# A five-layer graph network kernel: inputs loaded in small parts, own edges added by TensorE, the norm's low pieces by VectorE

## The chip, the cores and the metric

One core of a Trainium2 chip runs the whole program in one launch. The metric is the time of one execution on the device in microseconds (us), as the median of several runs. The core has five engines that run in parallel and meet at semaphores: TensorE (PE; its weight loads are shown apart as PEld), VectorE (DVE), ScalarE (ACT), GpSimd (POOL) and SyncE (SP, which here issues most of the DMAs).

## The reference, cut to what matters

```python
def _gin_conv(x, src, dst, edge_attr, w1, b1, bn_w, bn_b, w2, b2, ew, eb):
    edge_emb = edge_attr @ ew.T + eb
    n = x.shape[0]                                            # 3125 nodes, 128 features
    agg_x = jax.ops.segment_sum(x[src], dst, num_segments=n) + x
    agg_e = jax.ops.segment_sum(edge_emb, dst, num_segments=n) + eb
    h = jnp.concatenate([agg_x, agg_e], axis=1)
    h = h @ w1.T + b1                                         # 256 hidden
    mean = jnp.mean(h, axis=0)
    var = jnp.mean((h - mean) ** 2, axis=0)
    h = (h - mean) * jax.lax.rsqrt(var + BN_EPS) * bn_w + bn_b
    h = jax.nn.relu(h)
    return h @ w2.T + b2

h = jnp.maximum(_layernorm(x, axis=-1), 0.0)
for l in range(5):                                            # 103125 edges, sorted by dst, 16 attributes each
    h = _gin_conv(h, src, dst, edge_attr, W1[l], B1[l], BNW[l], BNB[l], W2[l], B2[l], EW[l], EB[l])
    if l < 4:
        h = jax.nn.relu(h)
return x + h
```

The `+ x` in `agg_x` is an edge of every node to itself on top of the listed ones. The text calls these the own edges.

## The kernel before

The kernel turns the edge list into a dense matrix of counts, `adj` (source node in 25 tiles of 128 rows, destination node in 3150 columns, bf16), and then aggregates by matrix products. The build comes first, in one block of the program, and is what the change touches. The five layers come after it and are not touched.

**Strips.** The columns of `adj` are built in 175 strips of 18 columns (`SC`), six groups of three columns each. For strip `u`, DVE makes two one-hot tables from the edge keys (`one_hots`, which calls `equal`, L421: a 128x768 form for the low part of the source node, a 128x456 form for the rest). PE multiplies them in six products into one of three PSUM banks (`counts`, L800). ACT copies the bank to `adj` (L935). The one-hot tables have two slots, so DVE's tables of strip `u` wait until PE's counts of strip `u-2` are done.

**Steps.** The edge attributes are summed by destination in 74 steps (`attr_step`, L824: 11 products, 22 instructions, since they are float32). DVE makes a one-hot table for each (`dst_one_hots`, L613). Step `u+6` (`LEAD`) is done in strip `u`, so the steps fill strips 0 to 67. The attributes lie in SBUF by 25 parts `k` of three steps each. Three times in each of seven chunks of 450 columns PE also splits the sums into pieces (L435, L439).

**The first norm.** ACT sums the rows of `x` (L962) from strip 7 on, squares from strip 20, and normalises from strip 36. Each group of four node tiles then gets a high piece in float16 (ACT, `high_piece`, L915) and a low piece, which is the value less the high piece (POOL, `low_piece`, L549, six of them; a seventh small one is DVE's, L745).

**Own edges and overflow.** POOL adds the identity to `adj` where a strip crosses the diagonal (`add_own`, L556, 31 pieces, bf16 from and to SBUF). It also adds the counts of overfull groups (`add_overflow`, L570, 14 of them). The first layer's aggregation (`agg0_products`, L430) is spread over strips 68 to 173 as 150 steps of a node tile each, one or two in a strip, and its last chunk runs after the last strip. It waits for both additions.

**Loading.** SP issues the DMAs in the order of its code. The attributes come in five parts (`ATTR_PARTS`), of 2, 2, 5, 7 and 9 of the 25 `k`, the node features `x` in one of 24 tiles and one for the rest, and all of it, with the weights, is issued without a wait once the first keys are loaded. After that SP stores the group starts (L478, L480), reads them back (L484), stores and reads the picks of the overfull groups (L486, L488), and loads the edge order for a check (L491). POOL issues the indirect gathers of edge rows and pairs (L528, L535).

The instructions of DVE, PE, ACT and POOL stand in the order of the code, strip by strip, so an engine that waits holds up all that is behind it.

## Time and profile before

| | |
|---|---|
| median of 3 runs | 686.85 us (686.78 to 686.87) |
| the profiled execution's own time | 684.61 us |
| its span, first to last instruction | 682.8 us |
| mean granted TensorE clock | 0.959 of full speed |

The profile is of one execution. Its span is 1.8 us shorter than its time, and its time is 2.2 us below the median of the three runs. Times in the rows are in microseconds from the span's start, and a busy PE is not PE at its peak. The build takes the first 245 us, the layers the rest.

### The profile page before, as it was taken

The numbers are of one execution on the slowest core, as the hardware profiler recorded it, in microseconds if no ns is written. First come the engines' busy times: TensorE is split into PE (matmuls) and PEld (weight loads), VectorE is DVE, ScalarE is ACT, GpSimd is POOL, SyncE is SP. The second block draws the span as 40 slices with busy tenths as digits, with TensorE's granted clock in tenths as the row PEclk, the third lists the DMA queues.
The fourth block names the chain that finished last, engine by engine and source line by source line (L and its number), as shares of the span: only waits on it lengthen the run. The fifth ranks groups of instructions, "written<-read, shape, count | busy, mean of one in ns | idle before, by whom it ended". The sixth has DMA issues, their size and how long they took to land.

```text
span 682.8 us, 13708 instructions
## 1 busy us (share of the span) xinstructions
PE 618.4 (91%) x5319; PEld 383.1 (56%) x5319; DVE 345.8 (51%) x837; ACT 262.5 (38%) x569; POOL 61.8 (9%) x90
## 2 busy tenths in 40 slices
PE   4788898988999979799997999997999998999976
PEld 3676677754555534755554755556655548555546
DVE  6788999989999937612112521204412125210124
ACT  1266966755666624701013510106201027010133
POOL 5640032410110100000000000000000000000000
PEclk9788999999999999999998999999999998999998
DMA  6961000000000000010000100000100000100033
GB/s 183 324 205 8 3 28 3 5 5 4 4 3 5 4 4 3 1 32 1 1 0 1 31 0 0 0 0 0 30 0 0 0 0 0 32 1 2 0 94 95
DMA packets 13305, 18.97 MB, mean 28 GB/s; under 512 B 2263, under 2 KB 7397, under 8 KB 13251
## 3 DMA queue, kind: packets, MB, share of 16 engines
q1 hardware_dynamic: 12099, 16.00, 7.7%
q0 software_dynamic: 1152, 2.20, 1.4%
q8 instruction: 40, 0.66, 0.4%
q14 instruction: 14, 0.11, 0.1%
HBM read 16.26 MB, written 1.60 MB: 26 GB/s over the span
## 4 chain that ended last, share of the span: by engine, by line
PE 57%; DVE 3%; ACT 1%; issue 1%; POOLq 0%; DVEq 0%
PE bank L1275 38%; PE bank L1338 10%; PE bank L1310 7%; PE bank L1304 2%; DVE bn_stats L1497 1%; ACT h L1391 1%; DVE h L1518 0%; ACT aggT L1382 0%; DVE h L1519 0%; PE bank L230 0%; ACT bn_small L1404 0%; PE bank L1321 0%; DVE h L1538 0%; DVE bound_row L1477 0%; DVE bn_small L1512 0%
## 5 line engine op out<-in xcount | busy, mean ns | idle before, releaser
L1275 PE MATMUL bank<-adj,h_pieces 128*128 (+1 forms) x1372 | 265.4, 353 | 0.0
L1275 PEld LDWEIGHTS bank<-adj,h_pieces 128*128 128x128 f16 x1372 | 133.1, 97 | 131.6 <-issue 8.7
L1497 DVE BATCH_NORM_STATS2 bn_stats<-bank 128x6 f32<-128x450 f32 (+1 forms) x70 | 43.8, 629 | 228.7 <-PE bank L1310 224.8
L935 ACT ACTIVATE adj<-bank 128x450 bf16<-128x450 f32 x175 | 96.0, 549 | 78.0 <-PE bank L800 63.2
L1382 ACT ACTIVATE aggT<-bank 128x450 f32<-128x450 f32 x28 | 15.3, 546 | 270.6 <-PE bank L1310 237.9
L421 DVE TENSOR_TENSOR h<-iota_lo,h 128x768 bf16<-128x768 bf16 (+1 forms) x182 | 101.6, 558 | 5.8 <-PE bank L800 4.4
L824 PE MATMUL bank<-h,adj 128*17 128x40 f32 (+11 forms) x1752 | 84.2, 207 | 15.7 <-DVE h L613 9.6
L824 PEld LDWEIGHTS bank<-h,adj 128*17 128x17 f32 x1752 | 73.0, 104 | 23.2 <-DVE h L613 13.2
L800 PEld LDWEIGHTS bank<-h 128*128 128x128 bf16 x1064 | 51.7, 100 | 60.6 <-DVE h L421 46.3
L800 PE MATMUL bank<-h 128*128 128x75 bf16 x1064 | 70.3, 203 | 16.6 <-DVE h L421 14.6
L430 PE MATMUL bank<-adj,h_pieces 128*128 128x450 bf16 x343 | 83.6, 356 | 1.6 <-issue 1.6
L1338 PE MATMUL bank<-weights,h 128*128 128x128 f32 (+1 forms) x500 | 65.8, 299 | 18.7 <-DVE h L1519 18.7
L1338 PEld LDWEIGHTS bank<-weights,h 128*128 128x128 f32 (+1 forms) x500 | 64.1, 212 | 22.8 <-issue 17.8
L421 DVE TENSOR_TENSOR h<-iota_a,key_a 128x456 bf16<-128x456 bf16 (+1 forms) x182 | 75.3, 414 | 0.0
L613 DVE TENSOR_TENSOR h<-h,adj 128x440 f32<-128x440 f32 x74 | 45.7, 619 | 8.3 <-remote 6.4
L1310 PE MATMUL bank<-aggT,weights 128*128 128x450 f32 x112 | 47.3, 544 | 1.0 <-ACT aggT L1382 1.0
L1391 ACT ACTIVATE h<-bank,weights 128x450 f32 (+1 forms) x70 | 41.4, 635 | 13.8 <-DVE bn_stats L1497 13.0
L1399 ACT ACTIVATE h<-h,bn_small 128x512 f32<-128x512 f32 (+1 forms) x65 | 44.3, 744 | 4.5 <-DVE bn_small L1513 4.5
L1525 DVE TENSOR_TENSOR h<-bank,weights 128x512 f32<-128x512 f32 x30 | 20.7, 691 | 34.6 <-PE bank L1338 34.6
L430 PEld LDWEIGHTS bank<-adj,h_pieces 128*128 128x128 f16 x343 | 27.3, 98 | 15.5 <-issue 3.1
L1310 PEld LDWEIGHTS bank<-aggT,weights 128*128 128x128 f32 x112 | 20.8, 189 | 15.7 <-issue 10.6
L556 POOL TENSOR_TENSOR adj<-adj,ident 128x128 bf16<-128x128 bf16 (+13 forms) x31 | 14.3, 466 | 116.8 <-ACT adj L935 116.8
(147 smaller groups left out, 323.1 us busy)
## 6 DMA issues: line engine op xcount, KB each, us to landing
adj<-attr SPq DMA_DIRECT2D x1, 2524.5 KB
adj<-attr SPq DMA_DIRECT2D x1, 1963.5 KB
weights<-wpack SPq DMA_DIRECT2D x5, 323.0 KB
out<-h SPq DMA_DIRECT2D x6, 256.0 KB
adj<-attr SPq DMA_DIRECT2D x1, 1402.5 KB, 6.8
adj<-attr SPq DMA_DIRECT2D x2, 561.0 KB
h<-mpack SPq DMA_DIRECT2D x5, 179.0 KB
adj<-order SPq DMA_DIRECT2D x2, 202.0 KB
```

The source lines that it names most:

```text
L421: return nc.vector.tensor_tensor(out.rearrange("p (j c t) -> p j c t", j=j, t=2), pairs.unsqueeze(1).to_broadcast([P, j, n // 2, 2]), key. ...
L430: last = nc.tensor.matmul(bank[:, 0:CW], hp[:, k, s, :], adj[:, k, ds(c * CW, CW)], start=(k == 0 and s == 0), stop=stop and s == pieces_o ...
L613: V.tensor_tensor(dst_oh[:, i % DST_SLOTS, :].rearrange("p (q w) -> p q w", q=RUN), iota_d.unsqueeze(1).to_broadcast([P, RUN, DW]), rel_d[ ...
L800: last = nc.tensor.matmul(cnt_ps[n % CNT_BANKS][:, g * AW:(g + 1) * AW], lo[:, g * P:(g + 1) * P], a[:, g * AP:g * AP + AW], start=(g == 0 ...
L824: last = nc.tensor.matmul(att_ps[c % 2][0:REC, a - c * CW:b - c * CW], attr_i[:, k, t * REC:(t + 1) * REC], dst_oh[:, i % DST_SLOTS, q * D ...
L935: nc.scalar.activation(out_view(u), bank_view(n % CNT_BANKS), ACT.Copy).then_inc(s_ev, 1)
L1275: last = nc.tensor.matmul(agg_ps[b][:, 0:CW], hp[:, k, s, :], adj[:, k, ds(c * CW, CW)], start=(k == 0 and s == 0), stop=stop and s == pie ...
L1310: nc.tensor.matmul(w1_ps[b][h][:, 0:CW], wp[:, W1A + h * P:W1A + (h + 1) * P], sums_in, start=False, stop=True).then_inc(w1_done, 1)
L1338: last = nc.tensor.matmul(w2_ps[u % 2][0:r, j * P:(j + 1) * P], h1[:, h, a:a + r], wp[:, W2T + h * P:W2T + (h + 1) * P], start=(h == 0), s ...
L1391: last = nc.scalar.activation(h1[:, h, ds(c * CW, CW)], w1_ps[b][h][:, 0:CW], ACT.Identity, bias=wp[:, B1 + h:B1 + h + 1])
L1399: last = nc.scalar.activation(v, v, ACT.Relu, bias=shift[:, h:h + 1], scale=scale[:, h:h + 1])
L1497: V.bn_stats(stats[:, h, ds(c * 6, 6)], w1_ps[b][h][:, 0:cols]).then_inc(st_last if last and h == 1 else st_done, 1)
```

## The change

The attributes are loaded in 13 parts of two `k` each (the last of one), each issued 12 steps ahead of its first use and behind a wait for that step. `x` is loaded in four parts of six tiles, at steps 6, 8, 10 and 12. The stores of the group starts come after step 24's part, the picks after strip 32's work, and the weights after all attribute parts. The own edges are one or two more products of PE in every strip: the identity times a shifted cut of a padded identity, 18 columns, accumulated into the same bank before ACT copies it. The six low pieces are DVE's, each two strips after its high piece. POOL has neither of the two any more.

```diff
-ATTR_PARTS = ((0, 2), (2, 4), (4, 9), (9, 16), (16, 25))
+ATTR_PARTS = [(k, min(k + 2, NODE_TILES)) for k in range(0, NODE_TILES, 2)]
+X_PARTS = ((0, 6), (6, 12), (12, 18), (18, 24))
-ORDER_AFTER = 9
+ORDER_AFTER, ATTR_AHEAD, X_EVERY, STARTS_AFTER = 9, 12, 2, 24
...
-        ident = sb(whole, "ident", [P, P], BF16)
+        ident_pad = sb(whole, "ident", [P, 2 * SC + P], BF16)
+        ident = ident_pad[:, SC:SC + P]
...
                     sp.wait_ge(s_pair[0], 16)
-                    attr_rows(2)
                     sp.wait_ge(s_zero, 1)
-                    sp.dma_start(x_st[:, 0:NODE_TILES - 1, :],
-                                 x[0:(NODE_TILES - 1) * P, :].rearrange("(k p) f -> p k f", p=P)).then_inc(s_x, 16)
                     sp.dma_start(x_st[0:LAST_ROWS, NODE_TILES - 1, :],
-                                 x[(NODE_TILES - 1) * P:N_NODES, :]).then_inc(s_x, 16)
-                    for m in range(3, len(ATTR_PARTS)):
-                        attr_rows(m)
+                                 x[(NODE_TILES - 1) * P:N_NODES, :]).then_inc(s_x[-1], 16)
+                    parts = 2
+                    for i in range(STEPS):
+
+                        if parts < len(ATTR_PARTS) and i == max(3 * ATTR_PARTS[parts][0] - ATTR_AHEAD, 0):
+                            if i > 0:
+                                sp.wait_ge(s_step, i)
+                            attr_rows(parts)
+                            parts += 1
+                        for j in range(len(X_PARTS)):
+                            if i == LEAD + X_EVERY * j:
+                                sp.wait_ge(s_step, i)
+                                x_rows(j)
+                        if i == STARTS_AFTER:
+                            store_starts()
+                        if i == PICK_AT + LEAD:
+                            spread_picks()
                     sp.dma_start(wp[:, :], wpack[0]).then_inc(l_wp, 16)
                     sp.dma_start(mp, mpack[0]).then_inc(l_mp, 16)
...
-                        if c == CHUNKS - 1:
-                            add_own(len(PIECES_OWN) - 1)
                         pool.wait_ge(s_ev, max(strip_at((c + 1) * CSTRIPS - 1), overflow_at(c)) + 1)
-                        pool.wait_ge(s_own, own_before(c))
...
-                        if u >= NORM_AT + 4 and (u - NORM_AT) % 4 == 0 and (u - NORM_AT) // 4 < UNITS:
-                            low_piece((u - NORM_AT) // 4 - 1)
-                        while n < len(PIECES_OWN) - 1 and PIECES_OWN[n][2] <= (u + 1) * SC:
-                            add_own(n)
-                            n += 1
...
+                        i = (u - NORM_AT - 6) // 4
+                        if (u - NORM_AT - 6) % 4 == 0 and 0 <= i < UNITS - 1:
+                            dve.wait_ge(s_hi, i + 1)
+                            V.tensor_tensor(units(hp, i)[:, :, 1, :], units(x_st, i), units(hp, i)[:, :, 0, :],
+                                            ALU.subtract).then_inc(hp_done, 1)
...
+                        if own is not None:
+
+                            to = cnt_ps[n % CNT_BANKS][:, 0:SG * AW].rearrange("p (g k m) -> p g k m", g=SG, m=GW)
+                            for k in range(own * SC // P, min((own * SC + SC - 1) // P, NODE_TILES - 1) + 1):
+                                at = SC + own * SC - k * P
+                                last = nc.tensor.matmul(to[:, :, k, :], ident, ident_pad[:, at:at + SC], start=False, stop=True,
+                                                        skip_group_check=True)
                         last.then_inc(s_cnt, 1)
...
-                        counts(strip_at(u), SG)
+                        counts(strip_at(u), SG, u)
...
                             if k == 0:
-                                pe.wait_ge(s_own, own_before(c))
                                 pe.wait_ge(s_ov, OV * (c + 1))
...
-                            if k == 0:
-                                act.wait_ge(s_x, 32)
+                            for j, (a, _) in enumerate(X_PARTS):
+                                if k == a:
+                                    act.wait_ge(s_x[j], 32 if j == len(X_PARTS) - 1 else 16)
```

SP's queue before, from its second attribute part to the picks:

```order
L457 DMA adj<-attr 128x2x561
L457 DMA adj<-attr 128x5x561
L467 DMA adj<-x 128x24x128
L469 DMA adj<-x 53x128
L457 DMA adj<-attr 128x7x561
L457 DMA adj<-attr 128x9x561
L473 DMA weights<-wpack 128x646
L474 DMA h<-mpack 128x358
L478 DMA starts<-start_index 60x1
L480 DMA starts<-start_index 126x1 x8
L484 DMA h<-starts 7x150 x2
```

The same queue now; the rows from the second of `adj<-attr 128x2x561 x2` on stand behind waits for steps:

```order
L442 DMA adj<-attr 128x2x561
L471 DMA adj<-x 53x128
L442 DMA adj<-attr 128x2x561 x2
L452 DMA adj<-x 128x6x128 x3
L442 DMA adj<-attr 128x2x561
L452 DMA adj<-x 128x6x128
L442 DMA adj<-attr 128x2x561 x2
L456 DMA starts<-start_index 60x1
L458 DMA starts<-start_index 126x1 x8
L462 DMA h<-starts 7x150 x2
L442 DMA adj<-attr 128x2x561 x2
```

The large transfers are cut up and spread, the stores of the starts stand behind more of them, and the weights behind all.

PE's queue before, in the part where the first layer's products (L430) share it with the counts (L800):

```order
L430 MATMUL bank<-adj,h_pieces 128x450 x4
L800 MATMUL bank<-h 128x75 [waits counts_evacuated,onehots_made]
L800 MATMUL bank<-h 128x75 x5
L430 MATMUL bank<-adj,h_pieces 128x450 x2
L800 MATMUL bank<-h 128x75 [waits counts_evacuated,onehots_made]
```

And now, where L783 is the counts, L791 the own edges and L415 the first layer:

```order
L783 MATMUL bank<-h 128x75 [waits counts_evacuated,onehots_made]
L783 MATMUL bank<-h 128x75 x5
L791 MATMUL bank<-ident 128x6x3
L415 MATMUL bank<-adj,h_pieces 128x450 x4
L783 MATMUL bank<-h 128x75 [waits counts_evacuated,onehots_made]
L783 MATMUL bank<-h 128x75 x5
L791 MATMUL bank<-ident 128x6x3 x2
L415 MATMUL bank<-adj,h_pieces 128x450 x2
```

Each strip has one own product more, and two where it crosses from one node tile to the next.

On DVE, around strip 42, where the first of the six low pieces (L724) now stands between a step's one-hots (L591) and the next strip's (L409):

```order
L409 TENSOR_TENSOR h<-iota_lo,h 128x768
L409 TENSOR_TENSOR h<-iota_a,key_a 128x456
L591 TENSOR_TENSOR h<-h,adj 128x440
L724 TENSOR_TENSOR h_pieces<-adj,h_pieces 128x4x128
L409 TENSOR_TENSOR h<-iota_lo,h 128x768
L409 TENSOR_TENSOR h<-iota_a,key_a 128x456
```

Before, the row L724 was not there and the others stood the same.

## Rows read from the trace of the kernel before

**Rows 1.** The page, busy time of each engine over the span.

```profile
PE 618.4 (91%) x5319; PEld 383.1 (56%) x5319; DVE 345.8 (51%) x837; ACT 262.5 (38%) x569; POOL 61.8 (9%) x90
```

**Rows 2.** Stretches: length, then busy time (instructions) of each engine, clock, DMA share, GB/s.

```profile
18.00:62.00 44.00, 36.51 (x590) 28.53 (x591) 34.53 (x97) 20.56 (x75) 19.85 (x17) 0.78 0.71 200
62.00:144.00 82.00, 73.27 (x1469) 60.87 (x1470) 79.59 (x195) 61.69 (x172) 19.93 (x21) 0.95 0.03 9
144.00:245.00 101.00, 91.81 (x976) 48.82 (x976) 96.83 (x244) 64.32 (x123) 12.83 (x30) 0.98 0.01 4
28.00:32.00 4.00, 2.25 (x24) 1.47 (x24) 0.00 (x0) 0.00 (x0) 2.62 (x3) 0.62 1.05 314
```

**Rows 3.** Waits of DVE from 17 to 245 us: total, times, longest.

```profile
DVE h L613 <- remote: 6.4, 2, 4.3
DVE h L421 <- PE bank L800: 4.4, 10, 0.9
DVE h L613 <- PE bank L824: 1.9, 3, 0.6
DVE h L421 <- issue: 1.0, 1, 1.0
```

**Rows 4.** Timeline, DVE's two long waits: start, duration, and idle before.

```profile
32.06 0.62 DVE L613 TENSOR_TENSOR h<-h,adj 128x440 f32<-128x440 f32 x1 [4.29 <-remote]
...
56.49 0.62 DVE L613 TENSOR_TENSOR h<-h,adj 128x440 f32<-128x440 f32 x1 [2.06 <-remote]
```

**Rows 5.** Groups of DVE by form, 17 to 245 us: busy, mean ns, idle before.

```profile
L421 DVE TENSOR_TENSOR h<-iota_lo,h 128x768 bf16<-128x768 bf16 x175 | 99.6, 569 | 5.4 <-PE bank L800 4.0 <-issue 1.0
L421 DVE TENSOR_TENSOR h<-iota_a,key_a 128x456 bf16<-128x456 bf16 x175 | 73.7, 421 | 0.0
```

**Rows 6.** Line L639 on the overflow keys: ns minimum/median/maximum of two.

```profile
L639 DVE TENSOR_SCALAR h<-h,picked_start_and_first x2: 270/747/1224, 105.5 to 105.7; 7x128 f32<-7x128 int32 x2
```

**Rows 7.** Timeline, DVE beside POOL's low piece, and beside an overflow addition.

```profile
100.39 1.43 POOL L549 TENSOR_TENSOR h_pieces<-adj,h_pieces 128x512 f16<-128x512 f32 x1 [7.95 <-ACT h_pieces L915]
...
100.75 1.32 DVE L421 TENSOR_TENSOR h<-iota_a,key_a 128x456 bf16<-128x456 bf16 x1
...
154.46 0.52 DVE L421 TENSOR_TENSOR h<-iota_a,key_a 128x456 bf16<-128x456 bf16 x1
```

**Rows 8.** Timeline of DVE, then of PE, two strips of the late part.

```profile
188.42 0.55 DVE L421 TENSOR_TENSOR h<-iota_lo,h 128x768 bf16<-128x768 bf16 x1
188.89 0.39 DVE L421 TENSOR_TENSOR h<-iota_a,key_a 128x456 bf16<-128x456 bf16 x1
189.20 0.55 DVE L421 TENSOR_TENSOR h<-iota_lo,h 128x768 bf16<-128x768 bf16 x1
...
188.79 0.92 PE L430 MATMUL bank<-adj,h_pieces 128*128 128x450 bf16 x4
189.55 0.37 PE L800 MATMUL bank<-h 128*128 128x75 bf16 x6
189.76 0.54 PE L430 MATMUL bank<-adj,h_pieces 128*128 128x450 bf16 x2
```

**Rows 9.** Timeline of DVE, one step's one-hots and what follows.

```profile
98.44 0.62 DVE L613 TENSOR_TENSOR h<-h,adj 128x440 f32<-128x440 f32 x1
98.98 0.55 DVE L421 TENSOR_TENSOR h<-iota_lo,h 128x768 bf16<-128x768 bf16 x1
```

**Rows 10.** Group of PE's counts, 17 to 245 us.

```profile
L800 PE MATMUL bank<-h 128*128 128x75 bf16 x1064 | 70.3, 203 | 16.6 <-DVE h L421 14.6 <-issue 0.8
```

**Rows 11.** Group of PE's counts' weight loads, 17 to 245 us.

```profile
L800 PEld LDWEIGHTS bank<-h 128*128 128x128 bf16 x1064 | 51.7, 100 | 60.6 <-DVE h L421 46.3 <-issue 3.7
```

**Rows 12.** Timeline of SP's queue: the starts stored, and read back; DVE's first use.

```profile
49.11 0.35 SPq L478 DMA_DIRECT2D starts<-start_index  x1
...
63.82 0.62 SPq L484 DMA_DIRECT2D h<-starts  x2
...
83.17 0.30 DVE L655 TENSOR_TENSOR h<-h 7x150 f32<-7x150 int32 x1
```

**Rows 13.** Timeline, end of the build: POOL's last own piece, overflow, PE's last chunk.

```profile
243.59 0.33 POOL L556 TENSOR_TENSOR adj<-adj,ident 128x78 bf16<-128x78 bf16 x1 [2.90 <-ACT adj L935]
244.17 0.75 POOL L570 TENSOR_TENSOR adj<-adj,h 128x75 bf16 x2 [0.24 <-POOL adj L556]
245.02 9.48 PE L430 MATMUL bank<-adj,h_pieces 128*128 128x450 bf16 x49 [1.60 <-issue]
```

More of the change, by code:

```diff
@@ L157, in ln_tiles @@
     return range(2 * (u - at), min(2 * (u - at) + 2, NODE_TILES)) if at <= u else ()
-def diag_pieces():
-    pieces = []
-    for k in range(NODE_TILES):
-        a, end = k * P, min((k + 1) * P, COLS)
-        while a < end:
-            b = min(end, (a // CW + 1) * CW)
-            pieces.append((k, a, b))
-            a = b
-    return pieces
 def agg0_steps(u):
@@ L378, in gin_program @@
             s_attr = [sem(f"attr_rows{m}_loaded") for m in range(len(ATTR_PARTS))]
-            s_x = sem("x_loaded")
+            s_x = [sem(f"x{j}_loaded") for j in range(len(X_PARTS))]
             s_zero = sem("x_pad_zeroed")
@@ L463, in _, with x_rows, store_starts @@
                     attr_rows(1)
+                    def x_rows(j):
+                        a, b = X_PARTS[j]
+                        sp.dma_start(x_st[:, a:b, :], x[a * P:b * P, :].rearrange("(k p) f -> p k f", p=P)).then_inc(s_x[j], 16)
+                    def store_starts():
+                        sp.wait_ge(s_start, BLOCKS)
+                        sp.dma_start(starts[0:BLOCK0].rearrange("(p b) -> p b", b=1), start_i[0:BLOCK0, 0:1]).then_inc(s_sdram, 16)
+                        for b in range(1, BLOCKS):
+                            sp.dma_start(starts[base_of(b):base_of(b) + GB].rearrange("(p b) -> p b", b=1),
+                                         start_i[0:GB, b:b + 1]).then_inc(s_sdram, 16)
+                        sp.wait_ge(s_sdram, 16 * BLOCKS)
+                        for at, out in ((0, first_e), (1, next_e)):
+                            sp.dma_start(out, starts[at:at + GROUPS].rearrange("(c j) -> c j", c=CHUNKS)).then_inc(s_ranges, 16)
@@ L473, in _ @@
+                    assert parts == len(ATTR_PARTS)
                     sp.dma_start(wp[:, :], wpack[0]).then_inc(l_wp, 16)
                     sp.dma_start(mp, mpack[0]).then_inc(l_mp, 16)
[L477 to L481 removed]
@@ L791, in transposes, with counts @@
                         last.then_inc(s_tr, 1)
-                    def counts(n, tiles):
+                    def counts(n, tiles, own=None):
                         pe.wait_ge(s_oh, n + 1)
```

40 lines of the change are left out of this document (8 added, 32 removed).

## The prediction

> **What bounds the kernel now.** I read the page's busy times first [rows 1], and they mislead: PE is busy 91% of the span, but most of that is in the layers, which the change leaves alone. So the view that counts is the table of stretches over the build, the first 245 us [rows 2]. From 62 to 144 us DVE is busy 79.59 of 82 us, from 144 to 245 us 96.83 of 101 us, while PE has 73.27 and 91.81. DVE sets the pace of the strips, and PE follows close behind. From 18 to 62 us it is otherwise: DVE has only 34.53 of 44 us, and the DMA share is 0.71. The list of DVE's waits says what it lacks there [rows 3]: 6.4 us in two waits that the profile calls remote, at 27.8 and 54.4 us in the timeline [rows 4]. Both are waits for PE's step, and PE itself waits there for nothing that the profile shows. From 28 to 32 us the DMA engines have no time free (share 1.05, 314 GB/s), PE gets 24 products done in 4 us, and DVE and ACT none [rows 2].
>
> So there are three kinds of time to be had or lost: the two stalls, what makes DVE's own instructions long, and PE's distance from being the bound.
>
> **Smaller parts in the queue.** Term A is the first stall. It costs 4.29 us [rows 4]. The clock then falls to the lower of its levels (0.62 in that stretch [rows 2], so partly at 1.2 GHz), and the knock-on is one wait of 1.0 us called issue and one of the three waits on L824, 0.6 us [rows 3]: 5.9 us. The change takes away what coincides with it. The parts now issued before strip 0 are 561 KB each in place of the 1.4 MB (5 `k`), 1.6 (`x`), 2.0 (7) and 2.5 (9) in one go, and nearly all behind a step. I take the stall as gone, −5.9 us; the other bound is 0, since the coincidence is all that the rows show.
>
> A page of the Trainium skill speaks against this cause: Runtime: NRT & Kernel Launch, section Instruction fetch mechanics, says that an engine streams its own instructions ahead by a DMA queue and that the cost of crossing a block is mostly hidden. By that the full DMA engines would not starve PE of instructions; the dribble of 24 products in 4 us [rows 2] does not fit a hidden fetch, but no row names it either. That is the rival "the stalls stay" below.
>
> Term B is the second stall, 2.06 us [rows 4] with a knock-on of about 0.5 us of the waits on L800 and 0.6 us on L824 [rows 3]: 3.2 us. It falls when SP stores the group starts, from 49.11 us on [rows 12], with the large transfers over. The change moves those stores some four strips later but doesn't remove them. Nothing tells me whether the stall goes; I take half, −1.6 us, with 0 and −3.2 as bounds.
>
> What the queue moves: the starts are stored after step 24 (strip 18), where before they went with strip 14. Store to read-back takes 63.82 − 49.11 = 14.7 us; DVE's first use is at 83.17 us [rows 12]. Strip 18's step ends at about 57 us [rows 4], so 26 us are left for these 14.7 and a landing: no wait. Every attribute part has 12 steps of at least 1.3 us each ahead of it (0.54 us for the step's one-hots [rows 9] and 0.78 for the strip's [rows 8]), against a transfer of 561 KB, 2 us at the rate of [rows 2]. Strips 18 to 32 take (83.17 − 56.49) / 14 = 1.9 us each [rows 4, 12], so the part due at step 30 goes out behind the store at about step 32 and has 10 steps left. The weights are needed only after the last strip. Cost 0, covered by that distance.
>
> **POOL's work leaves.** Term C. A DVE instruction that meets a POOL one that reads and writes SBUF gets longer: beside the low piece the 128x456 one-hot took 1.32 us [rows 7] in place of 0.39 [rows 8]. How much in all follows from the groups [rows 5] less the undisturbed durations [rows 8]: 99.6 − 175 × 0.55 = 3.35 us for the one form, 73.7 − 175 × 0.39 = 5.45 us for the other. L639 adds 1.22 − 0.27 = 0.95 us [rows 6]. That is 9.75 us. The 14 overflow additions stay, each 0.52 − 0.39 = 0.13 us [rows 7, 8], 1.8 us. So −8.0 us, on the engine that sets the pace. The bounds are −8.5 (L613 is stretched too now and then) and −5, if PE, which is co-bound in the late part, takes a part of it.
>
> **The low pieces on DVE.** The trace has no such instruction on DVE. The nearest is L613, float32 in SBUF, two inputs, 440 columns: the next starts 98.98 − 98.44 = 0.54 us after it [rows 9]. For 512 columns that is 0.54 × 512 / 440 = 0.63, less for the fixed part: 0.60 us, six times 3.6 us. Each waits for ACT's high piece, two strips earlier. The first one here begins at 100.39 − the 0.6 us of the high piece on ACT, and ends where POOL starts, 100.39 [rows 7]; DVE comes to that place at 98.98 + 1.3 = 100.3 us [rows 9], so 0.1 us of wait, and it is about the same or nothing at the others: 0.3 us in all. Together +3.9 us; bounds 3.0 and 6.
>
> **Own edges on PE.** Term D. 197 products more, 77 in strips 0 to 67 and 120 after. Their price has no row. The counts, also 128x128 bf16 weights, go at (189.76 − 189.55) / 6 = 0.035 us each with 75 columns [rows 8]; the own ones have 18 columns but load weights too, so I take 0.04. The upper bound is the whole duration of one, 0.203 us [rows 10]. In the late part PE's work in a strip is 0.21 us of counts and, with 294 products over 106 strips at (189.55 − 188.79) / 4 = 0.19 us, 0.53 us: 0.74 us against DVE's 189.20 − 188.42 = 0.78 us [rows 8]. With 1.13 × 0.04 it is 0.78 as well. The two engines are then level, and because one strip has four products and the next two, with only two one-hot slots between the engines, part of it shows. I take half of 120 × 0.04 = 4.8 us, 2.4 us, and a fifth of 77 × 0.04 early, where DVE has more in a strip: 0.6. Together +3.0 us; bounds 0 and 10.
>
> The Trainium skill would price this higher: TensorE: Matmul & The Clock Gate, section LDWEIGHTS, gives a weight load as its columns over 1.2 GHz, an estimate of 107 ns for 128 columns. By the page 0.107 would stand where I have 0.04, and the sum would come out nearly 7 us higher, since the groups' mean of 100 ns for a load [rows 11] overlaps the products but this price would not. Here six loads and products took 0.21 us together [rows 8], so the trace speaks against using it as a cost of each.
>
> **The end.** PE's last chunk waits for the overflow addition, which waits for the last own piece: from 243.59 to 244.17 us [rows 13]. −0.6 us.
>
> **Sum.** −5.9 − 1.6 − 8.0 + 3.9 + 3.0 − 0.6 = −9.2 us. The profiled execution took 684.61 us by its own time, so 675.4; it lies 2.24 us below the median of 686.85, and against that median the forecast is 677.6.
>
> **The rivals.**
> 1. *The forecast*, the sum above with B at either end: 676 to 679.3 by B alone. Chance 0.5.
> 2. *The stalls stay.* For: B falls without large transfers, so full DMA engines can't be the one cause of both, and PE's waits have no releaser. Against: the DMA share of 1.05 in the first. −9.2 + 5.9 + 1.6 = −1.7: 685.2. Chance 0.18.
> 3. *PE becomes the bound.* The own products cost p each, and PE's strip passes DVE's. The exposed cost is about 120p − (0.78 − 0.74) × 106 late and 77p − 5 early (0.08 us of room in 68 strips). Without them the sum is −12.2 us. At p = 0.1 that is 7.8 + 2.7 = 10.5 and the time is 685.2. Slower than before from p = 0.11 on; at the bound of 0.203 it would be 30.7 us, 705. For: PE is level with DVE already [rows 2]. Against: 0.035 us a product [rows 8]. Chance 0.09, of which 0.06 slower.
> 4. *All of it.* Both stalls go and PE's work is hidden: −9.2 − 1.6 − 3.0 = −13.8: 673.1. For: removing 2.9 us and more of stretched one-hots lets both engines flow. Chance 0.17.
> 5. *The queue is late.* SP stands in its store of the starts, or a part behind it lands late, and DVE or PE waits some 3 us: 680.6. The 11 us of distance speak against it. Chance 0.06.
>
> **How the numbers follow.** The likeliest is 677.6 us. From 672.5 to 685.3 the range takes in cases 1, 4 and 5 and the centres of 2 and of 3 at p = 0.1, and leaves out the slower end of 3 and the tails, under 0.2. A measurement of this kernel tells about 0.2% from no change, 1.4 us. Case 2 lies on the edge of that, so I give it 0.07 for no change, with 0.02 from the others: faster 0.84, same 0.09, slower 0.07.
>
> **What the profile would show.** A: from 20 to 45 us DMA share well under 1, no idle of DVE over 2 us before strip 7, and the clock not at its lower level there. B: whether a wait of DVE of about 2 us called remote is left when the starts are stored. C: the one-hots at 0.55 and 0.39 us on the mean, except beside 14 overflow additions; low pieces at 0.6 us. D: own products 0.04 us apart, DVE's waits for PE's counts up from 4.4 us by 2 to 3, strips in the late part still 0.78 to 0.83 us. The end: PE's wait before its last chunk 1.0 in place of 1.6 us. The layers take the same time as before. I would be wrong if PE's dribble has another cause than the transfers, or if the own products' price is 0.1 us.

## The result and the profile after

The changed kernel takes 684.22 us (median of 11 runs) beside 688.26 us for the kernel before on the same chip: a ratio of 0.9949, with a 95% interval of 0.9925 to 0.9973. In three more batches of runs the two kernels were timed side by side, and the ratios were 0.9935 [0.9913, 0.9956], 0.9950 [0.9927, 0.9972] and 0.9952 [0.9927, 0.9976]. (A batch here is a set of runs of several kernels taken together on one chip, with the kernel before among them; the recorded texts say "call". Times are compared within a batch.) So the change makes the kernel faster by half a per cent, some 3.5 us, where 9.2 us were forecast.

The page's busy times of the changed kernel, to be laid beside [rows 1]:

```profile
PE 621.1 (91%) x5516; PEld 394.6 (58%) x5516; DVE 341.2 (50%) x843; ACT 263.4 (39%) x569; POOL 43.3 (6%) x53
```

POOL has lost 18.5 us of work, and DVE, which has taken over six low pieces, is busy 4.6 us less than before all the same. The table of stretches of the same kernel, with the columns of [rows 2]:

```profile
18.00:62.00 44.00, 38.31 (x667) 31.82 (x668) 36.12 (x102) 23.16 (x84) 18.06 (x15) 0.81 0.45 128
62.00:144.00 82.00, 74.70 (x1520) 62.71 (x1521) 77.93 (x203) 61.72 (x169) 11.32 (x6) 0.96 0.19 54
144.00:245.00 101.00, 93.57 (x1070) 54.76 (x1069) 92.81 (x237) 62.25 (x119) 4.69 (x10) 0.97 0.02 4
28.00:32.00 4.00, 1.94 (x28) 1.38 (x27) 1.81 (x4) 1.09 (x3) 2.07 (x3) 0.73 0.59 180
```

The last line is the one to look at. The DMA share from 28 to 32 us has fallen from 1.05 to 0.59, as forecast, and still PE gets only 28 products done in those 4 us, against 24 before. PE's timeline there, with the idle time before each group and what ended it:

```profile
26.96 0.26 PE L814 MATMUL bank<-h,adj 128*17 128x28 f32 x4 [0.48 <-issue]
27.68 0.29 PE L814 MATMUL bank<-h,adj 128*17 128x24 f32 x5 [0.46 <-issue]
28.43 0.28 PE L814 MATMUL bank<-h,adj 128*17 128x20 f32 x5 [0.46 <-issue]
29.18 0.29 PE L814 MATMUL bank<-h,adj 128*17 128x24 f32 x5 [0.47 <-issue]
```

Five products, a gap of 0.46 us in which PE waits for nothing that the profile shows, and again: one round every 0.74 us. The text calls this a dribble. It is the first stall, still there. DVE's waits from 17 to 245 us, as in [rows 3]:

```profile
DVE h L409 <- PE bank L791: 6.0, 14, 1.2
DVE h L591 <- PE bank L814: 3.5, 5, 0.8
DVE h L591 <- remote: 3.2, 2, 1.8
DVE h L409 <- remote: 0.9, 1, 0.9
...
DVE h L409 <- PE bank L783: 0.6, 1, 0.6
```

They add up to 14.2 us, where those of [rows 3] add up to 13.7. The one wait of 4.29 us [rows 4] is cut up into four of 0.6 to 1.8 us between 26 and 34 us, but the total over the build hasn't moved. What did move is the length of DVE's instructions, in its groups by form (compare [rows 5]; L724 are the low pieces):

```profile
L409 DVE TENSOR_TENSOR h<-iota_lo,h 128x768 bf16<-128x768 bf16 x175 | 97.0, 554 | 7.5 <-PE bank L791 5.6 <-remote 0.9 <-PE bank L783 0.6
L409 DVE TENSOR_TENSOR h<-iota_a,key_a 128x456 bf16<-128x456 bf16 x175 | 68.6, 392 | 0.0
...
L724 DVE TENSOR_TENSOR h_pieces<-adj,h_pieces 128x512 f16<-128x512 f32 x6 | 4.1, 684 | 0.0
```

And the end of the build on PE (compare [rows 13]), with the first product of the layers:

```profile
240.38 9.49 PE L415 MATMUL bank<-adj,h_pieces 128*128 128x450 bf16 x49 [0.93 <-POOL adj L556]
255.24 0.91 PE L1294 MATMUL bank<-edge_sums,edge_weights 102*128 102x450 bf16 x2 [5.37 <-issue]
```

The last chunk begins 4.64 us earlier than before (245.02 us). But then PE stands still for 5.37 us before the layers' first product, where the kernel before stood still for 2.32. That row of the kernel before reads:

```profile
256.82 0.54 PE L1304 MATMUL bank<-edge_sums,edge_weights 102*128 102x450 bf16 x2 [2.32 <-POOL ones L1433]
```

So 3.05 us of the build's gain are given back at the border between the two blocks of the program, and only 1.58 us are left where the layers begin.

### The profile page after: what moved, and what is told of

It reads as the page before. It is cut to its first block, busy times and chain, and to the rows that moved or that the text cites. A ratio compares the mean times of both kernels' runs of the same rounds, so it can differ in the third digit from the quotient of the medians.

```text
span 683.5 us, 14077 instructions
## 1 busy us (share of the span) xinstructions
PE 621.1 (91%) x5516; PEld 394.6 (58%) x5516; DVE 341.2 (50%) x843; ACT 263.4 (39%) x569; POOL 43.3 (6%) x53
## 4 chain that ended last, share of the span: by engine, by line
PE 58%; DVE 3%; ACT 1%; issue 1%; POOLq 0%; DVEq 0%
PE bank L1265 38%; PE bank L1328 10%; PE bank L1300 7%; PE bank L1294 2%; DVE bn_stats L1487 1%; ACT h L1381 1%; DVE h L1508 0%; ACT aggT L1372 0%; DVE h L1509 0%; PE bank L220 0%; ACT bn_small L1394 0%; PE bank L1311 0%; DVE h L1528 0%; DVE bound_row L1467 0%; DVE bn_small L1502 0%
## 5 line engine op out<-in xcount | busy, mean ns | idle before, releaser
L409 DVE TENSOR_TENSOR h<-iota_lo,h 128x768 bf16<-128x768 bf16 (+1 forms) x182 | 99.0, 544 | 7.8 <-PE bank L791 6.0
L1328 PE MATMUL bank<-weights,h 128*128 128x128 f32 (+1 forms) x500 | 68.1, 306 | 18.7 <-DVE h L1509 18.7
L415 PE MATMUL bank<-adj,h_pieces 128*128 128x450 bf16 x343 | 84.3, 358 | 0.9 <-POOL adj L556 0.9
L783 PEld LDWEIGHTS bank<-h 128*128 128x128 bf16 x1064 | 54.3, 101 | 51.4 <-DVE h L409 34.0
L783 PE MATMUL bank<-h 128*128 128x75 bf16 x1064 | 70.3, 203 | 13.6 <-DVE h L409 12.2
L1328 PEld LDWEIGHTS bank<-weights,h 128*128 128x128 f32 (+1 forms) x500 | 66.4, 218 | 22.8 <-issue 17.8
L409 DVE TENSOR_TENSOR h<-iota_a,key_a 128x456 bf16<-128x456 bf16 (+1 forms) x182 | 70.3, 386 | 0.0
L591 DVE TENSOR_TENSOR h<-h,adj 128x440 f32<-128x440 f32 x74 | 45.2, 612 | 6.9 <-PE bank L814 3.5
L415 PEld LDWEIGHTS bank<-adj,h_pieces 128*128 128x128 f16 x343 | 26.2, 97 | 14.9 <-POOL adj L556 1.4
L791 PE MATMUL bank<-ident 128*128 128x18 bf16 x197 | 31.6, 177 | 0.0
```

Of the source, the lines that this page charges most:

```text
L409: return nc.vector.tensor_tensor(out.rearrange("p (j c t) -> p j c t", j=j, t=2), pairs.unsqueeze(1).to_broadcast([P, j, n // 2, 2]), key. ...
L415: last = nc.tensor.matmul(bank[:, 0:CW], hp[:, k, s, :], adj[:, k, ds(c * CW, CW)], start=(k == 0 and s == 0), stop=stop and s == pieces_o ...
L591: V.tensor_tensor(dst_oh[:, i % DST_SLOTS, :].rearrange("p (q w) -> p q w", q=RUN), iota_d.unsqueeze(1).to_broadcast([P, RUN, DW]), rel_d[ ...
L783: last = nc.tensor.matmul(cnt_ps[n % CNT_BANKS][:, g * AW:(g + 1) * AW], lo[:, g * P:(g + 1) * P], a[:, g * AP:g * AP + AW], start=(g == 0 ...
L1328: last = nc.tensor.matmul(w2_ps[u % 2][0:r, j * P:(j + 1) * P], h1[:, h, a:a + r], wp[:, W2T + h * P:W2T + (h + 1) * P], start=(h == 0), s ...
```

## The experiments

**One part at a time.** Four kernels, each the kernel before with some parts of the change. The first has the loading change alone (the diff shows its core), the second the own edges alone, the third the low pieces alone, the fourth the last two together.

```diff
 only_load
-ATTR_PARTS = ((0, 2), (2, 4), (4, 9), (9, 16), (16, 25))
+ATTR_PARTS = [(k, min(k + 2, NODE_TILES)) for k in range(0, NODE_TILES, 2)]
+X_PARTS = ((0, 6), (6, 12), (12, 18), (18, 24))
...
 only_own
-                            add_own(n)
...
+                                last = nc.tensor.matmul(to[:, :, k, :], ident, ident_pad[:, at:at + SC], start=False, stop=True,
...
 only_low
-                            low_piece((u - NORM_AT) // 4 - 1)
...
+                            V.tensor_tensor(units(hp, i)[:, :, 1, :], units(x_st, i), units(hp, i)[:, :, 0, :],
+                                            ALU.subtract).then_inc(hp_done, 1)
```

Expected of the loading alone: 

> Edit: of the change only the loading (attributes and x in parts, starts and picks later in the queue). The prediction's terms A and B: if the transfers starve PE, 7.5 us less than before. Rival, from the trace of the changed kernel (PE still dribbles near 27 us with the DMA share at 0.54, and DVE loses 7.4 us near it): the loading is worth nothing, within 1.5 us of before, and the first stall stands in the trace in the same place.

Of the own edges alone: 

> Edit: of the change only the own edges as products on PE, none on POOL. Prediction: 31 stretched one-hots of about 0.2 us less (near 5 us), PE's work visible by 3.0 us, the end 0.6 us: 2 to 3 us less. If each own product costs 0.1 us: 5 us more than before. If 0.04 us and hidden: 5 us less.

Of the low pieces alone: 

> Edit: of the change only the six low pieces on DVE. Prediction: five stretched one-hots of 0.93 us and a smaller one less, six times 0.65 us more: 1.0 us less than before. If DVE waits for ACT's high pieces: the same or slower, with waits for L915 in the trace.

Of the last two together: 

> Edit: the whole change but the loading. If the loading is worth nothing or costs time (theory now): as fast as the whole change or up to 2 us faster, some 4 us less than before. If the loading saves the stalls (the prediction's A and B): 7.5 us slower than the whole change.

Here the kernel before took 678.06 us (35 runs), not 688. Loading alone took 682.65 us, ratio 1.0049 [1.0020, 1.0077]; own edges alone 679.28, 1.0008 [0.9983, 1.0032]; low pieces alone 674.40, 0.9946 [0.9920, 0.9972]; both 677.25, 0.9974 [0.9949, 0.9999]. By these ratios the loading costs 3.3 us, where 7.5 us less or no more than 1.5 us either way was expected; the own edges give nothing, where 2 to 3 us were expected; the low pieces give 3.7 us, where 1.0 was expected; and the last two give 1.8, where some 4 were expected. So none of the four came out as written down. None of the four has the dribble, whatever its transfers; PE's largest single gap of this kind before strip 24 is 1.21 us, in the fourth. Stretches of the kernel with the low pieces alone, which keeps the old, large transfers:

```profile
28.00:32.00 4.00, 3.32 (x57) 2.29 (x55) 3.91 (x11) 1.29 (x3) 3.00 (x3) 1.00 1.05 323
32.00:40.00 8.00, 7.38 (x161) 6.51 (x161) 7.78 (x25) 7.77 (x32) 4.41 (x4) 1.00 1.06 335
```

The DMA share is 1.05, exactly that of the kernel before, and PE does 57 products in place of 24. A full DMA system is neither needed for the stall (the changed kernel) nor enough for it (this one). Nor are POOL's gathers of edge rows enough: five of them go out one every 1.3 to 1.5 us from 25.2 to 31.6 us here too. The tables below compare where these kernels stand at fixed places.

**The same kernels again.** To see whether the stall belongs to the kernels or to the occasion, both kernels were run unchanged beside each other, with two padded ones. The padding is idle products at the start of PE's program.

```diff
 low_pad197 (the low pieces on DVE, and)
+                    pe.wait_ge(s_ident, 1)
+                    for _ in range(197):
+                        nc.tensor.matmul(stack_ps[0:P, 0:18], ident[:, :], ident[:, 0:18], start=True, stop=True, skip_group_check=True)
                     for i in range(LEAD):
```

For the kernel before, the text was: 

> The kernel before, unchanged, on the chip of the other kernels of this call, for its profile. Theory 1 (the first stall is of the kernel: its large transfers or POOL's burst of row gathers): DVE's wait of 4.3 us near 28 us and the one of 2.1 us near 54 us are there again. Theory 2 (the stalls are of the chip or of the placement of the program in memory, since none of the four partial kernels showed one of over 1.3 us): no wait of DVE over 1.3 us before strip 24, which then begins near 60 us in place of 67.8, and a span some 7 us shorter. Ratio 1.000 either way.

For the changed kernel: 

> The changed kernel, unchanged, on the same chip as the kernel before beside it. Theory 1: seven gaps of PE of 0.46 us near 27 to 31 us and strip 24 at 65.8 us again. Theory 2: no such gaps, strip 24 near 58 us, and its gain over before without the stalls shows as the build's 4 to 5 us less 3 us of PE's late start into the layers: ratio 0.996 to 0.999. In both the layers' first product waits 5.4 us behind the last chunk.

For the first padded kernel: 

> The kernel before with the low pieces on DVE, and 197 idle 18-column products of the identity at the very start of PE's program (none in the strips; they run while PE waits for the first keys, in some 8 us). It gives PE the same number of instructions as own edges do. Theory P (PE's late start into the layers, 5.3 us in place of 2.3 in every kernel with own edges, comes from how many instructions stand ahead of it on PE, so from their supply): 5.3 us here too, total about 677 us. Theory Q (it comes from the own edges' own work or waits): 2.3 us as in the kernel with the low pieces alone, ratio 0.995.

For the second, the changed kernel with 64 idle products: 

> The changed kernel with 64 idle 18-column products more at the start of PE's program, 128 instructions. Theory P: the place where PE runs dry shifts or changes; PE's start into the layers is other than 5.4 us (between 2.3 and 5.4), and gaps of PE called issue lie elsewhere than in the changed kernel. Theory Q: 5.4 us again and the same gaps at the same strips, time within 0.2% of the changed kernel.

The kernel before took 688.39 us in this batch (687.08, 1.0000 [0.9973, 1.0028], as a kernel of its own), the changed one 683.77 (0.9935). The dribble is there in both; PE's second gap is 1.41 us in the kernel before and 0.48 in the changed one. Theory 2 is right that the stall isn't the kernel's alone, and its forecast for this batch was wrong, since the stall had come back. Stretches of the kernel before, to be laid beside those of the kernel with the low pieces:

```profile
28.00:32.00 4.00, 2.10 (x22) 1.38 (x20) 0.07 (x1) 0.22 (x1) 2.93 (x3) 0.64 1.06 316
32.00:40.00 8.00, 7.72 (x84) 5.70 (x83) 5.63 (x14) 3.56 (x10) 1.00 (x1) 0.50 1.05 346
```

And the kernel with the low pieces alone once more, the same program, from the next batch, where the kernel before took 686.98 us:

```profile
28.00:32.00 4.00, 2.24 (x27) 1.47 (x27) 0.20 (x1) 0.35 (x2) 3.06 (x3) 0.86 1.05 325
```

The same program and the same share, 27 products in place of 57: the stall comes and goes with nothing changed in the kernel. And from 32 to 40 us, when the dribble is over and PE is busy 7.72 of 8 us, the granted clock is at its lower level (1.2 GHz), 0.50 in place of 1.00. In all three profiles of the kernel before it is 0.50 to 0.55 there. Over 18 to 62 us the clock is 0.78 [rows 2], against 0.96 in the kernel with the low pieces alone. This low clock after the stall is a part of its price; in the prediction's 5.9 us it stands only as the two knock-on waits.

The first padded kernel took 687.55 us, ratio 0.9994 [0.9974, 1.0013]: 197 idle products at the start of PE's program cost all that the low pieces gain. They weren't quite free where they ran, from 2.73 to 9.8 us: strip 0 begins at 19.3 us, where the profiles of the kernel before have 17.8 to 18.1. The row at the border:

```profile
256.70 0.53 PE L1310 MATMUL bank<-edge_sums,edge_weights 102*128 102x450 bf16 x1 [5.67 <-issue]
```

5.67 us, as in the changed kernel, without an own edge in any strip. The late start into the layers therefore comes with instructions added ahead of it on PE, whatever they do (theory P). The second padded kernel, 683.11 us, 0.9919 [0.9889, 0.9949], has 5.42 us there, which is what theory Q had for it: past 197 products, 64 more change nothing. At which number it tips wasn't found. And the number on PE isn't all: the kernel with the loading alone adds no instruction to PE, starts into the layers after the usual 2.32 us, and has a gap of the same kind, 2.50 us, one group of products later (251.50 us, shown below).

**Spacing POOL's gathers.** In the trace the first stall lies beside POOL's burst of seven row gathers. In two kernels the gathers of block 2 to 8 wait for a step each.

```diff
                         pool.wait_ge(s_lidx, min(b, 2) + 1)
+                        if b >= 2:
+                            pool.wait_ge(s_step, b + 6)
```

Of the kernel before with it: 

> The kernel before, with POOL's gathers of edge rows spread out: the gather of block 2 to 8 waits for the sums of step 8 to 14, where before the last five go out one every 1.3 us from 25 to 31.5 us. Theory G (the first stall, PE's gaps of 0.46 us from 27 to 31 us, comes from this burst of gathers, which ends when it ends): on a chip where the kernel before takes about 688 us the stall is gone or shorter than 1.3 us, the low clock from 40 to 53 us with it, and the time is 5 to 8 us shorter; where it takes about 678 us, 0 to 1 us shorter. Theory H (the stall is a property of the chip that has nothing to do with the gathers): same stall at the same time, ratio 1.000.

Of the changed one: 

> The changed kernel with the same spreading of the gathers. Theory G: no gaps of PE of 0.4 us or more between 27 and 32 us, and where before takes about 688 us some 5 us less than the changed kernel. Theory H: the seven gaps are there again, time within 0.2% of the changed kernel.

Beside them ran the changed kernel, 

> The changed kernel, unchanged, beside the others of this call. If this is a chip on which before takes about 678 us: theory 2 (the stalls are the chip's) expects no seven gaps, strip 24 near 58 us, and a time of 677 to 681 us, so that the change is worth nothing or loses there (its loading change alone lost 0.5%). If before takes about 688 us: 683.8 again, ratio 0.9935.

and the low pieces alone: 

> The kernel before with the low pieces on DVE alone, once more, for the other chip. If before takes about 688 us here: theory 2 expects the stalls in it too, and a gain of the same 3 to 4 us as before (ratio 0.994 to 0.996). If before takes about 678 us: ratio 0.9946 again.

The kernel before took 686.98 us. The low pieces alone took 684.34, 0.9954 [0.9930, 0.9979], the whole change 682.97, 0.9950 [0.9927, 0.9972]. Spaced gathers gave 684.45 for the kernel before, 0.9977 [0.9955, 1.0000], and 681.78 for the changed one, 0.9938 [0.9922, 0.9954], which is not to be told from the change alone. PE's gaps in the kernel before with spaced gathers:

```profile
35.76 0.38 PE L802 MATMUL bank<-h 128*128 128x75 bf16 x6 [0.35 <-issue]
...
38.04 0.20 PE L826 MATMUL bank<-h,adj 128*17 128x40 f32 x1 [0.46 <-issue]
...
40.96 0.36 PE L826 MATMUL bank<-h,adj 128*17 128x40 f32 x3 [0.38 <-issue]
41.69 0.97 PE L826 MATMUL bank<-h,adj 128*17 128x40 f32 x12 [0.37 <-issue]
...
54.78 1.43 PE L826 MATMUL bank<-h,adj 128*17 128x40 f32 x19 [3.06 <-issue]
```

And POOL's timeline in the same kernel:

```profile
35.81 1.29 POOL L537 DMA_INDIRECT adj<-pair,start_index  x1 [0.30 <-issue]
37.40 1.07 POOL L537 DMA_INDIRECT adj<-pair,start_index  x1 [0.30 <-issue]
38.78 1.00 POOL L537 DMA_INDIRECT adj<-pair,start_index  x1 [0.30 <-issue]
40.32 1.05 POOL L537 DMA_INDIRECT adj<-pair,start_index  x1 [0.54 <-issue]
```

The dribble has left 27 to 32 us and lies at 35 to 42 us, under the pair gathers, which now stand back to back. The stretch that it left, with the large transfers unchanged:

```profile
28.00:32.00 4.00, 3.76 (x65) 2.60 (x62) 3.08 (x8) 1.94 (x4) 2.78 (x3) 1.00 1.05 314
```

65 products at a DMA share of 1.05, in a batch in which the kernel before has the stall: the share isn't what makes it. Strip 12 begins 3 to 5 us earlier than in the three profiles of the kernel before, at 39.9 us. Then PE's second gap is 3.06 us in place of 1.27 to 2.14, and strip 24 begins at 67.0 us, against 67.8. The changed kernel with spaced gathers has 2.70 us there, in place of 0.34 to 1.44. So most of what was won at strip 12 was lost again by strip 24, and the 1.6 us that the kernel before gains in time have an interval that ends at no change.

**Spreading everything.** If runs of small descriptors were the cause, spreading both gathers and the stores of the starts should have cleared all.

```diff
-    return b + 6 if b >= 2 else -1
+    return 2 * b + 8 if b >= 2 else -1
...
+                            pool.wait_ge(s_step, 2 * b + 9)
...
-                    sp.wait_ge(s_start, BLOCKS)
+                    sp.wait_ge(s_start, 1)
...
+                        sp.wait_ge(s_start, b + 1)
```

The kernel with the stores alone spread has, besides its two lines for `s_start`, a wait of SP for step `2 * b + 14` before each store.

Of the kernel before with it: 

> The kernel before with all its small descriptors spread: the row gather of block 2 to 8 behind step 13, 15 to 25, its starts computed in strip 12, 14 to 24 and its pair gather behind them, and the starts of each block stored when they are there instead of all nine in one go. Theory G (PE's dribbles without a releaser go with runs of small-descriptor DMAs: with POOL's gathers back to back, since spacing the row gathers moved the first dribble from 27-32 us to 36-42 us, where the pair gathers now stood back to back; and with the nine stores of the starts): no gap of PE called issue over 0.4 us from 20 to 75 us, clock not at its lower level from 40 to 53 us, strip 24 near 59 us in place of 67.8, and 6 to 9 us less where before takes about 688. Theory H (the dribbles only need traffic of any kind, or none): they show up again somewhere between 25 and 70 us, strip 24 at 65 us or later, ratio 0.995 to 1.000.

With the low pieces on DVE: 

> The same spreading, and the low pieces on DVE. Theory G: 6 to 9 us of the dribbles and 3 to 4 us of the low pieces, ratio 0.983 to 0.987 where before takes about 688 us. Theory H: the low pieces' part alone, 0.993 to 0.996.

Of the changed kernel with it: 

> The changed kernel with the same spreading of gathers and stores. Theory G: its stalls of 7 us go, 4 to 7 us below the changed kernel's 0.9935 to 0.995, so a ratio of 0.985 to 0.989. Theory H: 0.993 to 0.996.

Of the stores alone, in the kernel before: 

> The kernel before with only the stores of the starts spread: block 0 at once, block 1 to 8 behind step 16, 18 to 30, each 0.5 KB in 126 pieces of four bytes. Theory G: PE's first stall near 28 us as before, the second one (PE waits 1.4 to 2.1 us near 56 us, DVE 1.5 to 2.1) gone, and 1.5 to 3.2 us less, ratio 0.995 to 0.998. Theory H: a wait of PE of 1 us or more is still there between 50 and 70 us, ratio 1.000.

In this batch the kernel before took 679.19 us. The three spread kernels took 686.99, 684.89 and 685.86 us: ratios 1.0105 [1.0074, 1.0137], 1.0066 [1.0036, 1.0096] and 1.0096 [1.0067, 1.0124]. They are slower than what they spread, so theory G fails as a recipe. Whether spreading would clear the stalls where they stand wasn't tested, since the kernel before took the short time in this batch and the stand-in for it below has no gap of PE over 0.67 us; the spread kernels have gaps of PE of their own, up to 1.60, 1.23 and 1.25 us. Part of the loss is new waits of DVE, here of the first of them:

```profile
DVE adj L635 <- DMA adj<-dst_lin,row_index: 4.1, 3, 2.7
DVE adj L642 <- DMA adj<-pair,start_index: 0.8, 1, 0.8
```

Beside the kernel with the stores alone, that first one is 2.8 us behind at strip 24 (62.2 and 59.4 us), 5.2 at strip 68, 5.5 at strip 174 and 7.3 at the layers' first product, so most of its 8 us lies in the strips with steps; what it is there beyond the waits above isn't shown. The stores alone changed nothing: 678.32 us, 0.9996 [0.9971, 1.0021]. The largest gap of PE there from 20 to 75 us that no row explains is 0.67 us, so this kernel stands in the table for the kernel before without the stalls, which has no profile of its own in such a batch.

**The last two.** The changed kernel and the kernel before once more. 

> The changed kernel once more, in the hope of a call in which the kernel before takes 678 to 679 us. There its profile should have no dribble of PE near 28 us and no lower clock from 40 to 53 us. Theory 3 (the change is worth little without the stalls: 4 to 5 us in the build, less 3 us of PE's late start into the layers, less what the loading change costs there): 676 to 681 us, ratio 0.997 to 1.003. Its rival (the build's gain is all there, as the low pieces' 3.7 us were): 672 to 675 us, ratio under 0.995. If before takes 687 to 688 us: 683 again, ratio 0.993 to 0.996.

> The kernel before, for its profile in this call. If its median is 678 to 679 us: no stall of DVE over 1.3 us at 28 and at 54 us, strip 24 near 59 us in place of 67.8, the layers' first product near 249 us in place of 257. If it is 687 to 688 us: as in the profile before. Ratio 1.000 in both.

The kernel before took 687.37 us in this batch, so the short time that was wanted didn't come. The changed kernel took 684.63 us, 0.9952 [0.9927, 0.9976], with seven gaps of PE of 0.39 to 0.51 us from 27.2 to 31.6 us. The other was the kernel before again, 687.83 us, 0.9990 [0.9967, 1.0012]. The whole change was therefore never timed in a batch in which the kernel before takes 678 us. An estimate from the parts measured there is 0.9974 times 1.0049, so 1.002: no gain.

Where the kernels stand, in us of the timelines: the start of DVE's one-hots of three strips, the layers' first product, and the span. With the kernel before at 687 to 688 us:

| | strip 24 | strip 68 | strip 174 | first product | span |
|---|---|---|---|---|---|
| before, mean of 3 profiles | 67.8 | 143.3 | 241.9 | 257.6 | 684.9 |
| after, mean of 4 profiles | 65.7 | 138.5 | 235.8 | 253.5 | 682.0 |
| low pieces alone | 66.8 | 141.6 | 240.3 | 255.5 | 683.6 |

With the kernel before at 678 to 679 us, one profile each (that of the low pieces alone is of a run of 678.18 us, the longest of its twelve, whose median is 674.40, so its row is late for this kernel):

| | strip 24 | strip 68 | strip 174 | first product | span |
|---|---|---|---|---|---|
| stores spread (before) | 59.4 | 135.4 | 234.5 | 249.6 | 676.0 |
| loading alone | 58.1 | 134.1 | 233.3 | 248.5 | 680.6 |
| own edges alone | 58.6 | 133.5 | 231.4 | 249.0 | 677.2 |
| low pieces alone | 59.6 | 134.3 | 233.0 | 248.2 | 676.3 |
| own edges and low pieces | 58.4 | 130.8 | 228.3 | 246.0 | 676.2 |

The two tables differ by 8.4 us at strip 24 for the kernel before (67.8 and 59.4) and by about the same at every later place. At strip 6 the two are level (26.9 to 27.6 us and 27.2), so the whole difference between 678 and 687 us comes up between strips 6 and 24, where the stalls and the low clock after them lie. The low pieces' own gain is not placed: 3.2 to 3.7 us by the times, 1.5 to 2.2 us at the first product in these profiles.

## Why the prediction was wrong

The direction, faster, and the range held; the size was more than twice the measured one. The nearest case was the second rival, the stalls stay.

**Term A is the step that failed:** "The change takes away what coincides with it. [...] I take the stall as gone, −5.9 us". It measured 0. DVE's waits total 14.2 us against 13.7, and the stall is in all four profiles of the changed kernel. The DMA share did fall, to 0.59, so the step before it was right; that the stall follows from the share was the error. The kernel with the low pieces alone showed a share of 1.05 without a stall in one batch and with it in another. What decides is something that differs from batch to batch and that no kernel here sets: the kernel before took 678.06 and 679.19 us in two batches, and 686.98 to 688.39 us in four. It isn't the chip by its number either, since chips 10 and 14 each had a batch of both kinds (678.06 and 686.98, 679.19 and 688.39). In the batches with the stall it goes along with POOL's gathers when these are moved. The first padded kernel has the same gaps, 0.47 and 0.46 us, among its idle products at 8.1 and 8.9 us, beside two gathers at 6.1 and 7.5 us and at a DMA share of 0.22. But the kernel with the low pieces alone had its row gathers from 25.2 to 31.6 us without the dribble. Why PE stalls so, and what differs between batches, stays open. The prediction had the sign of this in hand: [rows 4] shows a second stall at 54 us, with the large transfers over, and one cause was still taken for the first. The price wasn't the error: A and B whole are 5.9 + 3.2 = 9.1 us, and at strip 24 the kernel before is 8.4 us later with the stalls than its stand-in without.

The Trainium skill (Runtime: NRT & Kernel Launch, section Instruction fetch mechanics) had been weighed there: it calls the cost of crossing a boundary in the instruction stream mostly hidden. The traces agree so far that full DMA engines alone don't starve PE (57 and 65 products at a share of 1.05). Whether the 3 us at the border of the program's blocks are a fetch no row says, so they speak neither for nor against it.

**Term B** may have come out near the half that was taken. PE's gap behind the stores of the starts was 2.14, 1.41 and 1.27 us in three profiles of the kernel before, and 1.44, 0.48, 0.34 and 0.55 us in four of the changed one: means of 1.61 and 0.70 us, 0.9 less. As a term by itself it isn't shown: the same gap is 1.53 us in the kernel with the low pieces alone and 1.97 in the first padded one, both with the old loading, but 2.70 in the changed kernel with spaced gathers, and the stores alone were only spread where there was no stall.

**Term C** was right. The one-hots' groups fell from 99.6 + 73.7 [rows 5] to 97.0 + 68.6 us, 7.7 us, and the overflow keys' two instructions from 1.49 [rows 6] to 0.54 us: 8.65 us in all against 8.0. The Trainium skill has the rule (SBUF — State Buffer, section SBUF: two separate sides): when VectorE reads two inputs in SBUF and GpSimd reads SBUF as well, one of them holds a shared pair of ports for its whole instruction and the other is blocked. [Rows 7] agree, 1.32 us beside a POOL instruction of 1.43.

**The low pieces** were priced right: 0.684 us each, the next instruction 0.61 us behind (99.96 to 100.57 us in DVE's timeline), so 3.7 us, and no wait of note.

**Term D** was the right amount in the wrong place, and that the amounts agree is luck. What comes after an own product starts 0.03 us behind it, in PE's timeline of the changed kernel:

```profile
189.27 0.38 PE L783 MATMUL bank<-h 128*128 128x75 bf16 x6
189.49 0.17 PE L791 MATMUL bank<-ident 128*128 128x18 bf16 x1
189.52 0.73 PE L415 MATMUL bank<-adj,h_pieces 128*128 128x450 bf16 x3
```

In the strips they show at most as DVE's waits for the counts, 6.0 + 0.6 in place of 4.4 us, which is what the prediction gave as a sign. In the second table the kernel with own edges alone is 3.0 us ahead of the kernel before at strip 174 and only 0.7 us ahead at the layers' first product. The 394 instructions (197 products and their loads) cost some 3 us at the border of the blocks: 5.27 to 5.69 us behind the last chunk in all ten profiles with them, 2.32 to 2.35 us in those without. The prediction's sentence "The layers take the same time as before" looked past this border, and no term stood for it. One sum in that part is off, too: a price of 0.107 us for each own product, put at nearly 7 us more, gives 5.1 us more with the prediction's own shares, a half of 120 and a fifth of 77.

**The end** gave 0.67 us (1.60 to 0.93), as forecast with 0.6.

With 0 for A the forecast's own sum is −3.3 us, and the measured change is −3.5 us (the ratio 0.9949 times 686.85 us). That agreement is partly luck: at strip 174 the changed kernel is 6.2 us ahead on the mean, the border takes back 3.1, and the layers, which aren't touched, are 1.2 us longer (428.5 against 427.3 us, where single profiles of one kernel differ by 2.3). The low pieces alone give 0.9954 beside 0.9950 for the whole change; what the own edges gain in the build goes at the border, and the loading change, alone, cost 0.5%. Of that loss the build shows nothing (it is 1.2 us ahead at the first product); it lies in the layers, 432.1 us against 426.4 in one profile each. Rows of their first 45 us place it, the kernel with the loading alone first, then the one with the stores spread, each with PE's first row behind the layers' first product:

```profile
251.50 3.37 PE L1330 MATMUL bank<-h,weights 128*128 128x450 f32 x4 [2.50 <-issue]
250.00:295.00 45.00, 39.58 (x193) 26.22 (x194) 22.45 (x48) 21.31 (x35) 0.00 (x0) 0.85 0.04 13
```

```profile
250.01 2.38 PE L1312 MATMUL bank<-h,weights 128*128 128x450 f32 x4
250.00:295.00 45.00, 40.63 (x218) 25.28 (x218) 26.04 (x59) 21.76 (x36) 0.00 (x0) 0.96 0.05 13
```

PE stands still for 2.50 us behind the first product, and the granted clock is 0.85 in place of 0.96; from 295 us on it is 0.97 in both. The layers' length in the other profiles goes with the same clock: 426.0 us where it is 0.96 in this stretch (the first profile of the kernel before), 428.2 at 0.92 (its second), 430.0 at 0.85 (the fourth of the changed kernel). Why it is lower in some is open, and with it why the loading change brings the gap.

## What to carry to other kernels

A stall that coincides with full DMA engines isn't yet caused by them: before it is booked as a gain, look for a second stall of the same kind where they are idle, and let a partial kernel show it gone. A gap whose releaser reads "issue" may come and go between batches of runs with the same program, so profile the kernel before in each batch and compare only within it. Moving work off GpSimd when VectorE sets the pace pays by the length of VectorE's own instructions (8.65 us here), which the groups by form show directly. But count the instructions that a change adds to an engine ahead of a block's border, even where they cost nothing at their place.

## What the runs showed of the hardware

- PE can be held to 4 or 5 products every 0.74 us, with gaps of 0.46 us that no semaphore explains. The same program (the low pieces alone) shows 57 products from 28 to 32 us in one batch and 27 in another, at a DMA share of 1.05 in both.
- With 197 idle products at the start of PE's program, done before the first strip, PE's gap before its first product in the next block was 5.67 us in place of 2.32.
- Six counts of 75 columns and one own product of 18, each with 128x128 weights of its own, take 0.25 us together (189.27 to 189.52 us), 0.036 us each, and the own one alone 0.03 us (189.49 to 189.52).
- After such a stall the granted clock was at its lower level (0.50) from 32 to 40 us, though PE was busy 7.72 of these 8 us; without the stall it was 1.00 there.
- The five layers, the same code in all kernels, took 426.0 us with a granted clock of 0.96 from 250 to 295 us and 430.0 us with 0.85 there, while it was 0.97 from 295 to 670 us in both.
